# Where epsilon is added in the four-layer graph network's normalisations: VectorE instead of GpSimd

## The reference

```python
def _layernorm(x, axis=-1, eps=1e-05):
    m = jnp.mean(x, axis=axis, keepdims=True)
    v = jnp.var(x, axis=axis, keepdims=True)
    return (x - m) / jnp.sqrt(v + eps)

x = _layernorm(x + _L0_gnn_ref(x, ...))     # graph attention, elu
x = _layernorm(x + _L1_gnn_ref(x, ...))     # adj @ x @ weight + bias
x = _layernorm(x + _L2_gnn_ref(x, ...))     # 8-head masked attention; in it: o + rsqrt-normalised o
x = _layernorm(x + _L3_gnn_ref(x, ...))     # three gated recurrent steps
```

## Time and profile before

| | us |
|---|---|
| median of 3 runs | 1406.11 |
| the three runs | 1404.98, 1406.11, 1406.47 |
| the profiled execution | 1405.35 |
| its span in the profile | 1403.2 |
| DVE busy | 1059.0 (75%) |
| ACT busy | 791.4 (56%) |
| POOL busy | 143.4 (10%) |

### The profile page before, as it was taken

The page is one execution under the profiler, slowest core; times in us unless marked ns, Lnnn a source line. Parts: engine busy times, 40 slices in busy tenths (PEclk is TensorE's granted clock), DMA queues, the critical chain, the costliest instruction groups (busy, mean ns, idle before and its releaser), DMA issues.

```text
span 1403.2 us, 26776 instructions
## 1 busy us (share of the span) xinstructions
PE 1337.7 (95%) x10357; PEld 1134.0 (81%) x10357; DVE 1059.0 (75%) x2367; ACT 791.4 (56%) x1450; POOL 143.4 (10%) x196
## 2 busy tenths in 40 slices
PE   5788999999999999999999999999999999999896
PEld 4677888888888888888888888888888887888784
DVE  5787778787787878778777777878878786868455
ACT  3555565656565565656566655655665555564453
POOL 4200100100010110001011010011001010100000
PEclk9899999999999999999999999999999999999998
DMA  5000010000000001000000001000000100000000
GB/s 174 1 24 24 1 24 31 21 32 15 7 30 22 30 15 37 0 22 30 22 30 15 22 15 22 30 22 30 15 7 30 23 31 9 31 8 31 16 1 30
DMA packets 54653, 34.52 MB, mean 25 GB/s; under 512 B 34896, under 2 KB 51536, under 8 KB 54608
## 3 DMA queue, kind: packets, MB, share of 16 engines
q1 hardware_dynamic: 52800, 29.43, 7.0%
q0 software_dynamic: 1248, 3.94, 0.9%
q10 hardware_dynamic: 560, 0.52, 0.1%
HBM read 12.92 MB, written 8.39 MB: 15 GB/s over the span
## 4 chain that ended last, share of the span: by engine, by line
PE 68%; DVE 16%; ACT 8%; issue 4%; POOL 3%; DMA 0%; ACTq 0%; POOLq 0%; DVEq 0%
PE banks L121 16%; PE banks L123 15%; PE banks L122 15%; PE banks L587 8%; PE banks L582 3%; ACT y L273 2%; PE banks L746 2%; PE banks L650 2%; PE banks L731 2%; PE banks L720 2%; DVE l_stats L245 2%; PE banks L848 1%; DVE l_r L2401 1%; DVE l_r L2394 1%; DVE l_sum L2241 1%
## 5 line engine op out<-in xcount | busy, mean ns | idle before, releaser
L1501 ACT ACTIVATE l_r<-banks,bias_r 128x512 f32<-128x512 f32 x90 | 61.7, 687 | 178.3 <-PE banks L123 178.2
L259 POOL TENSOR_TENSOR l_rstd<-l_mv,eps 128x4 f32<-128x4 f32 x48 | 25.8, 538 | 891.5 <-DVE l_mv L253 891.5
L1518 ACT ACTIVATE banks<-banks,bias_h 128x512 f32<-128x512 f32 x96 | 63.2, 659 | 64.7 <-PE banks L123 64.7
L2140 DVE TENSOR_TENSOR l_rh_lo<-l_r,l_rh_hi 128x512 fp32r<-128x512 f32 x90 | 61.7, 688 | 28.3 <-ACT l_rh_hi L1367 28.1
L2401 DVE SCALAR_TENSOR_TENSOR l_r<-banks,l_r 128x512 f32<-128x512 f32 x90 | 61.7, 687 | 26.4 <-ACT banks L1512 24.6
L1512 ACT ACTIVATE banks<-banks,bias_z 128x512 f32<-128x512 f32 x96 | 63.3, 659 | 26.3 <-PE banks L123 26.2
L273 ACT ACTIVATE y<-l_sum,l_offset,l_rstd 128x256 f32<-128x256 f32 x128 | 70.8, 594 | 12.0 <-DVE l_offset L267 11.1
L587 PE MATMUL banks<-adj_t,y 128*128 128x128 f32 x544 | 72.1, 283 | 4.3 <-ACT y L273 4.3
L587 PEld LDWEIGHTS banks<-adj_t,y 128*128 128x128 f32 x544 | 67.4, 197 | 8.3 <-ACT y L273 5.1
L121 PE MATMUL banks<-l_rh_hi,u_hi 128*128 128x512 f32 x180 | 73.6, 409 | 0.0
L2383 DVE SCALAR_TENSOR_TENSOR l_r<-l_r,l_h 128x512 f32<-128x512 f32 x60 | 40.8, 683 | 41.2 <-ACT l_r L1501 41.2
(11 more groups left out here) (294 smaller groups left out, 4354.6 us busy)
## 6 DMA issues: line engine op xcount, KB each, us to landing
x_tok<-in_x_dram SPq DMA_DIRECT2D x15, 512.0 KB, 3.5
l_res<-y SPq DMA_DIRECT2D x15, 512.0 KB, 2.9
out_dram<-l_res SPq DMA_DIRECT2D x15, 512.0 KB, 3.0
l_vpair<-l_vstage SPq DMA_DIRECT2D x32, 128.0 KB, 3.2
w_raw<-in_L_gnn_w_w_dram POOLq DMA_DIRECT2D x3, 512.0 KB, 7.7
qkv_raw<-in_L_gnn_w_qkv_dram POOLq DMA_DIRECT2D x1, 768.0 KB, 4.5
l_res<-in_x_dram SPq DMA_DIRECT2D x1, 512.0 KB, 5.1
u_raw<-in_L_gnn_u_w_dram POOLq DMA_DIRECT2D x2, 256.0 KB, 7.5
```

The lines of the kernel that those rows point to most:

```text
L1501: nc.scalar.activation(own(u).r[:, m, :], rz(u)[:, m, :], ACT.Tanh, scale=0.5, bias=w.biases["r"][:, m:m + 1]).then_inc(s.r_ready.of(u), 1)
L1518: nc.scalar.activation(hv(u)[:, m, :], hv(u)[:, m, :], ACT.Tanh, bias=w.biases["h"][:, m:m + 1]).then_inc(s.hv_ready.of(u), 1)
L2140: return nc.vector.tensor_tensor(parts[1][:, k, :], bank, parts[0][:, k, :].bitcast(F32), ALU.subtract)
```

## The change

`aggregate` no longer signals POOL with the last bn_aggr. That instruction raises a new semaphore `aggregated`; DVE waits for it itself, adds epsilon in place to the four variances (a tensor_scalar of 128x4 elements, stride 2), and signals POOL with that. `root` on POOL reads the sum and keeps only the power. The constant tile of epsilons and its memset go, and so does the semaphore between POOL's two operations.

```diff
-        self.eps = sb("eps", [P, TILES])
...
-        nc.gpsimd.memset(p.eps[:, :], EPS)
...
-        self.eps_added = Signal(p, f"{name}_eps_added", 1)
+        self.aggregated = Signal(p, f"{name}_aggregated", 1)
...
-        ins.then_inc(self.var_ready.sem, 1)
+        ins.then_inc(self.aggregated.sem, 1)
+        dve.wait_ge(*self.aggregated.at(u, 1))
+        nc.vector.tensor_scalar(self.mv[:, :, 1], self.mv[:, :, 1], EPS, None, ALU.add).then_inc(self.var_ready.sem, 1)
...
-        nc.gpsimd.tensor_tensor(self.rstd[:, :], self.mv[:, :, 1], self.p.eps[:, :],
-                                ALU.add).then_inc(self.eps_added.sem, 1)
-        pool.wait_ge(*self.eps_added.at(u, 1))
-        nc.gpsimd.tensor_tensor(self.rstd[:, :], self.rstd[:, :], self.p.minus_half[:, :],
+        nc.gpsimd.tensor_tensor(self.rstd[:, :], self.mv[:, :, 1], self.p.minus_half[:, :],
                                 ALU.pow).then_inc(self.rstd_ready.sem, 1)
```

## The result

The kernel before took 1405.97 us as the median of 21 runs beside it (1403.64 to 1407.19), the changed kernel 1407.91, likewise of 21 (the fastest 1406.67). One of these 21 took 1491.5 us at a mean granted clock of 0.843 instead of 0.986, in a slower state of the chip, and is left out of the ratio. By the medians the change costs 1.9 us; the ratio of 1.0017, with a 95% interval of 1.0011 to 1.0023, puts it at 2.4 us, between 1.5 and 3.2. So it is a slowdown clear of zero, about as large as the 0.2% (2.8 us) that the prediction took for what can be told from no change. The profiled execution has a span of 1405.5 us where the one before has 1403.2. DVE is busy 1072.8 us instead of 1059.0, POOL 125.6 instead of 143.4. The 13.8 us more on DVE are nearly all the 80 additions of 0.17 us (13.6), of which only a part reaches the end of the kernel.

A forecast was written before the change was run, and what follows sets the result against it. PE was taken as the bound, busy 82.29 of 83.09 us a pass, so only its waits count. 0.19 us times 11 passes (2.1), less 0.4 at the ends, made +1.7 and 1407.8 us; range 1404.4 to 1411.0.

The forecast's parts named there:

- The push at `l2i`: At the `l2i` norm: DVE's queue is pushed back 0.20 us, reaching `late_lo` and making PE 0.20 later.
- `y2`: Behind the `l2o` norm: the blocked power ends at 565.82 against 565.67, so `y2` and PE come 0.15 us later.
- `l1`: At the `l1` norm: the late second half of `l_h_lo` costs PE another 0.12 us, together 0.27.
- `l0`: At the `l0` norm: the root comes 0.08 us earlier, giving PE back 0.08 at its wait at 611.00.
- The powers: On POOL: powers of about 1.4 us at `l2o` and 1.9 at `l0`; DVE's wait near 0.9 instead of 1.18.
- The pass: One pass of the loop: 83.28 us, 0.19 more than before, times 11 passes 2.1 us.
- The ends: Fill and drain: some five norms alone on the serial path at either end give 0.08 us each, 0.4 together.
- the slower one: Rival: DVE's restart behind its wait takes 0.17 us; 0.42 a pass, 4.6 us, 1410.3 with the ends; chance 0.27.
- The faster one: Rival: the addition hides in DVE's queue and costs 0.08 us; 0.31 a pass gained, 1402.3 us; chance 0.07.
- the free wait: Rival: DVE's wait costs nothing, only the addition's own 0.16 us; zero a pass, 1405.7 with the ends; chance 0.11.
- The slack rival: Rival: `late_lo`, `l_h_lo` and `y2` do not hold PE up; only 0.08 at `l0` counts, 1404.8 us; chance 0.10.

The follow-up runs named there:

- e4: The change in the norms `l2i` and `l1` only, the others as in the kernel before: 1408.32 us, ratio 1.0021.
- e6: Changed kernel with a one-element memset on DVE behind the wait instead of the addition, epsilon left out: 1405.25 us, 0.9997 of the kernel before.
- e2: Kernel before, with DVE also waiting for its own bn_aggr and adding zero; POOL keeps both operations: 1416.57 us, ratio 1.0073.
- e9: Kernel before with two loop moves alone, `l2_base` behind the `l0` offset and `l3_reset` behind the `l2o` offset: 1399.52 us, ratio 0.9958.
- e7: Kernel before with epsilon as a constant third bn_stats triple, POOL keeping the power alone; variances not checked: 1398.37 us, ratio 0.9948.
- e8: e7 with the two moves of e9: 1394.64 us, 0.9919 of the kernel before.

## Why the prediction was right, point by point

The forecast of 1407.8 us (+1.7 against 1406.11) stands beside 1407.91 (+1.9 against 1405.97). That the two agree to 0.1 us is partly luck, since the base was 0.14 us off and the terms of the pass and of the ends erred in opposite directions; that the pass grows by 0.2 us, and through which waits, was foreseen. Its steps:

- **The push at `l2i`.** Predicted 0.20, found 0.23 at PE (0.69 us of idle time instead of 0.46). The addition starts 0.03 us behind the last bn_aggr's end and takes 0.17 (predicted 0.04 and 0.16), but what follows starts 0.08 to 0.11 behind it and itself lasts longer: `l_r` 0.69 instead of 0.66, `l_sum` 1.23 instead of 1.19. That last part was not in the sum, and the push is more than the distance between starts. Why the follower lasts longer stays open: it starts 0.06 to 0.09 us ahead of the recorded end of the operation before it in the changed kernel and 0.08 before, so the overlap does not tell them apart. At `l2o` it is 0.22 + 0.03 = 0.25, predicted 0.22.
- **`y2`.** Predicted +0.15 together, found +0.20. The power's 0.86 us behind the blocking operation were right (0.87), the larger push made the rest.
- **`l1`.** Predicted +0.27 together, found +0.26. The step that it took, +0.12, was +0.06, since more had been lost at `y2`. What set the place is when `l_h_lo` arrives on DVE. It was forecast for 583.98 at PE; less the 0.40 with which the pass begins, it was 583.97. DVE's push was larger there, too: the first half of `l_h_lo` ended 0.45 us later within the pass (at 581.63, before at 580.78), and not 0.37. But before the change `l_s` had waited for ACT's `l_h`, which ended at 580.75, and started at 580.78 without the overlap of 0.08; after it, `l_s` starts at 581.55 and waits for nothing. Those 0.08 took up the rest of the push. By the end of the pass little of this place is left, as e4 shows.
- **`l0`.** Predicted -0.08, found -0.08 at PE (0.26, then 0.18). The idle time there shrank from 0.94 to 0.87. It had been forecast to shrink by 0.3: PE's own lateness of 0.26 was to be hidden in it, but DVE and ACT come late by the same 0.26, since they had met PE before. The step of the sum was right; the sign by which it was to be recognised was not.
- **The powers.** Predicted 1.4 and 1.9 us and a wait of 0.9 on DVE; found 1.41, 1.92 and 0.90. DVE's waits for POOL over the whole span, before and after (us in total, times, longest):

```profile
DVE l_offset L267 <- POOL l_rstd L262: 19.7, 17, 1.4
DVE l2o_offset L267 <- POOL l2o_rstd L262: 15.0, 14, 1.2
```

```profile
DVE l_offset L264 <- POOL l_rstd L259: 14.9, 17, 1.1
...
DVE l2o_offset L264 <- POOL l2o_rstd L259: 11.1, 13, 0.9
```

  8.7 us less waiting for POOL, and the kernel is slower. DVE pays the wait at itself and the addition in its place.
- **The pass.** Predicted 83.28 us and +0.19; found 83.23 and +0.17 by the ten passes.
- **The ends.** Predicted -0.4; found +0.4 by the profiles and 0.0 by the medians. The profile of the change is 0.3 ahead at the loop's start, gains 0.5 more in the early drain, and loses some 0.5 twice towards 1300. This term was mis-sized, and one profile can't settle by how much (last section). It was the weakest of the sum.

The rivals: the slower one (+0.42 a pass) is out by the +0.17, and by the row at 564.72: `l_r` starts 0.11 us behind the addition, not 0.17. The faster one and the free wait forecast the power's end at `l2o` 0.11 us sooner or 0.05 later; it was 0.20 later. e6 speaks against the free wait, too: a wait with a 59 ns memset behind it moved DVE's queue by 0.16 us at `l2i` and 0.22 at `l2o`. The Trainium skill, "VectorE: DVE Perf Modes", section "The DRAIN you can't avoid", says of a chain of DVE operations that the semaphore costs nothing extra there, and that an operation which is not held starts before the pipeline is empty. The overlap of 0.08 us agrees with the second; with the first, taken over to a wait of DVE for its own last instruction, e6 does not agree. The slack rival is out by e2 and e4; in the changed kernel DVE ends `late_lo` 0.23 us later within the pass (564.28 against 563.65, less 0.40), and PE follows by 0.23.

## What to carry to other kernels

Moving an instruction from an engine with 10% load to one with 75% does not pay by the first engine's waits getting shorter: list where the receiving engine's queue feeds the bound one, and count the push at each, also where nobody waits for the moved result. A wait of an engine for its own last instruction is not free: with the issue of one small instruction it made 0.16 of the 0.23 us here at `l2i`, and all of the 0.22 at `l2o`. Look first for an order that takes the shared block off the chain (e9: 6.1 us) and for a way in which the operation vanishes (e7: 7.1 us, if the variances are right). Together they gave 10.8 us, less than their sum, where the change cost 1.9. And split each median into passes and ends before calling an expectation right: e2 and e8 hit by their ends, not by their passes.

## What the runs showed of the hardware

**A POOL operation slips in between two DVE operations.** In the drain two blocking operations of `l_r` stand back to back. In the kernel before, the addition had waited for the first and the power then waited for the second, 1.42 us. In the changed kernel (timeline, DVE and POOL):

```profile
1147.60 1.29 DVE L2380 SCALAR_TENSOR_TENSOR l_r<-l_r,l_h 128x512 f32<-128x512 f32 x2
...
1147.77 1.38 POOL L259 TENSOR_TENSOR l2o_rstd<-l2o_mv,minus_half 128x4 f32<-128x4 f32 x1 [6.87 <-DVE l2o_mv L254]
```

The power ends at 1149.15, only 0.26 us behind the second one's end (1148.89). The first of the two ends near 1148.29, if it lasts 0.69 us as `l_r` does at 564.72, and 0.86 behind that is 1149.15. So by the 0.86 us that the power needs behind a block it was let in behind the first, while the second was on: here the block lasted for one operation, and POOL needed no gap in DVE's queue. This is worked out from the ends, not seen. From `l_r`'s start to the power's end it was 2.22 us before (1145.82 to 1148.04) and is 1.55 now; less the push of 0.25 that is 0.4 us, most of what the drain first gained.

The loop has a second case, in the changed kernel at the `l1` norm, where `l_h_lo` and `l_s` stand back to back (timeline, DVE and POOL):

```profile
580.94 0.69 DVE L2137 TENSOR_TENSOR l_h_lo<-l_h,l_h_hi 128x512 fp32r<-128x512 f32 x1
...
581.09 1.41 POOL L259 TENSOR_TENSOR l_rstd<-l_mv,minus_half 128x4 f32<-128x4 f32 x1 [14.81 <-DVE l_mv L254]
...
581.55 0.42 DVE L2163 TENSOR_TENSOR l_s<-ident,l_h 128x256 f32<-128x256 f32 x1
```

The power ends at 582.50, 0.87 us behind `l_h_lo` (581.63) and only 0.53 behind `l_s` (581.97).

**Stretches of low granted clock cost more than the term that was to be measured, and they differ from profile to profile.** The stretch around 1300 us, where PE is half idle: busy us of PE, PEld, DVE, ACT, POOL, then the granted clock, in the kernel before:

```profile
1300.00:1305.00 5.00, 2.66 (x13) 2.66 (x14) 2.98 (x6) 3.61 (x7) 0.61 (x1) 0.75 0.12 48
1305.00:1310.00 5.00, 5.00 (x37) 4.74 (x36) 1.98 (x4) 2.44 (x5) 0.00 (x0) 0.91 0.16 62
```

In the changed kernel, a microsecond later:

```profile
1301.00:1306.00 5.00, 2.01 (x10) 2.01 (x11) 3.46 (x7) 3.08 (x7) 0.96 (x1) 0.59 0.00 2
1306.00:1311.00 5.00, 5.00 (x34) 4.96 (x33) 1.46 (x3) 1.77 (x4) 0.00 (x0) 0.73 0.27 108
```

The clock falls from 2.4 to 1.2 GHz for part of each, behind some 4 us in which PE did nothing, and stays low longer in the changed one; PE, 1.6 us behind at the head of this stretch, is some 0.5 more behind at its end. The fill varies likewise: e9 has the code of the kernel before there, and reaches the load of `mask_bias` that opens the attention scores at 197.43 where the kernel before reaches it at 195.75. Of these 1.7 us it has 0.6 already at 80 us (80.85 against 80.26 at the load of `l_s`); the rest comes between 82 and 86 us, where its granted clock is 0.69 and then 0.50, and 1.00 before. Terms of the ends below 2 us therefore can't be read from one profile each; the loop's can, and the medians over the runs carry the rest.
